# Projecting raw x in fp32 with centred weights in the first mixing stage of a hybrid layer

## The reference

```python
def _layernorm(x, axis=-1, eps=1e-05):
    m = jnp.mean(x, axis=axis, keepdims=True)
    v = jnp.var(x, axis=axis, keepdims=True)
    return (x - m) / jnp.sqrt(v + eps)

def _L0_attn_a_ref(x, W_q, W_k, W_v):
    Q = _l2norm(jnp.einsum('bnd,ed->bne', x, W_q))
    K = _l2norm(jnp.einsum('bnd,ed->bne', x, W_k))
    V = jnp.einsum('bnd,ed->bne', x, W_v)
    C = x.shape[1]
    global_feat = jnp.sum(K * V, axis=1, keepdims=True) / C
    return Q * global_feat

x = x + _L0_attn_a_ref(_layernorm(x, axis=-1), W_q, W_k, W_v)
x = x + _L0_ffn_ref(_layernorm(x, axis=-1), ...)
```

## Time and profile before

| what | us |
|---|---|
| median of 3 runs | 855.74 |
| lowest and highest run | 854.48, 856.68 |
| span of the profiled execution | 854.0 |
| TensorE busy (share) | 695.8 (81%) |
| VectorE busy | 576.9 (68%) |
| ScalarE busy | 515.5 (60%) |
| GpSimd busy | 480.7 (56%) |
| mean granted TensorE clock | 0.898 |

### The profile page before, as it was taken

One profiled execution on the slowest core, in us unless ns is written; L12 is line 12 of the kernel. 1 busy time (PEld: TensorE's weight loads), 2 busy tenths in 40 slices (PEclk: granted clock), 3 DMA queues, 4 the chain that ended last, 5 costly groups with the idle time before them and its releaser, 6 DMA issues.

```text
span 854.0 us, 22244 instructions
## 1 busy us (share of the span) xinstructions
PE 695.8 (81%) x7583; PEld 486.2 (57%) x7583; DVE 576.9 (68%) x1269; ACT 515.5 (60%) x1268; POOL 480.7 (56%) x501
## 2 busy tenths in 40 slices
PE   0663697898999957978898989988869798888888
PEld 0432686788888822333343434433238687877778
DVE  6699893766777376746986888975344256776646
ACT  3864874666666424746785878866453466766632
POOL 4995604677772478555177572166664336767640
PEclk9998599899999965887997999997568899999999
DMA  6222301232334142122122222121112212222217
GB/s 195 75 74 43 100 1 29 59 84 80 83 81 65 39 129 63 46 76 62 57 67 75 73 58 63 58 70 44 50 43 80 63 46 71 84 76 76 72 45 263
DMA packets 75810, 62.35 MB, mean 73 GB/s; under 512 B 11059, under 2 KB 68059, under 8 KB 75720
## 3 DMA queue, kind: packets, MB, share of 16 engines
q1 hardware_dynamic: 66632, 43.10, 17.6%
q0 software_dynamic: 9088, 17.98, 7.8%
HBM read 35.14 MB, written 26.68 MB: 72 GB/s over the span
## 4 chain that ended last, share of the span: by engine, by line
PE 52%; DVE 16%; ACT 10%; issue 8%; another core or an unknown queue 4%; DMA 3%; POOL 3%; SPq 1%; ACTq 0%; DVEq 0%; POOLq 0%
PE ps L995 25%; PE ps L1139 7%; PE ps L1382 7%; DVE mx L2431 5%; PE ps L1154 5%; ACT h L1591 3%; PE ps L1395 3%; DMA gy<-rows 2%; PE ps L1179 2%; POOL gy L840 2%; ACT xn L1504 1%; DVE xres L1903 1%; DVE stats L1813 1%; PE ps L1358 1%
## 5 line engine op out<-in xcount | busy, mean ns | idle before, releaser
L2431 DVE TENSOR_REDUCE mx<-ps 128x2 f32<-128x512 f32 x256 | 169.8, 684 | 62.5 <-PE ps L995 52.7
L1591 ACT ACTIVATE h<-ps,b1T 128x256 f32<-128x256 f32 x440 | 171.7, 478 | 59.3 <-PE ps L995 43.1
L1718 ACT ACTIVATE scratch<-ps 128x512 f32<-128x512 f32 x256 | 147.9, 599 | 71.4 <-PE ps L995 58.6
L995 PE MATMUL ps<-qkst 32*128 32x256 f16 x1024 | 112.6, 298 | 34.2 <-DVE mx L2431 23.6
L995 PE MATMUL ps<-xg,w1s 128*128 128x256 f16 x936 | 117.4, 276 | 23.4 <-issue 18.7
L799 POOL DMA_INDIRECT scratch<-rows,tok_i x78 | 90.3, 1157 | 70.6 <-DVE tok_i L2216 35.3
L942 POOL DMA_INDIRECT ytok<-yst,didx x78 | 92.1, 1181 | 58.1 <-DVE yst L2246 37.1
L1139 PE MATMUL ps<-w2s,hhi 128*128 x1248 | 118.6, 220 | 2.8 <-issue 1.7
L995 PEld LDWEIGHTS ps<-xg,w1s 128*128 x936 | 87.7, 99 | 38.3 <-issue 27.7
L1617 ACT ACTIVATE xg<-ps 128x512 f16<-128x512 f16 x78 | 46.5, 597 | 94.9 <-PE ps L1179 63.2
L2186 DVE SCALAR_TENSOR_TENSOR hlo<-h,hhi 128x1024 f16<-128x1024 f32 x78 | 95.6, 1225 | 2.7
(11 more groups left out here) (303 smaller groups left out, 1152.5 us busy)
## 6 DMA issues: line engine op xcount, KB each, us to landing
qkst<-qk SPq DMA_DIRECT2D x32, 256.0 KB
gy<-rows SPq DMA_DIRECT2D x39, 136.0 KB
ysorted<-yst SPq DMA_DIRECT2D x39, 128.0 KB
h<-in_L_ffn_ew SPq DMA_DIRECT2D x16, 256.0 KB, 3.1
qk<-hhi SPq DMA_DIRECT2D x32, 128.0 KB
xres<-in_L_attn_a_x SPq DMA_DIRECT2D x4, 512.0 KB, 6.1
rows<-hl SPq DMA_DIRECT2D x4, 512.0 KB, 3.1
qk<-hhi SPq DMA_DIRECT2D x32, 64.0 KB
```

What stands on the lines that cost most here:

```text
L995: return pe.matmul(o, a, b, start=start, stop=stop)
L1591: last = act.activation(h32[:, u % 2, f], HB[u % 2][:, f], ACT.Gelu_apprx_tanh, bias=b1T[:, ds(e * CH + c, 1)], scale=1.0 / PS)
L1718: act.activation(prb[:, (s // 4 * 4 + (s + 2) % 4) % 8, :], ps[:, s % 2, :], ACT.Exp, scale=HD ** -0.5 / (PS * PS))\
L2431: dve.tensor_reduce(mx[:, c, j:j + 2], ps[:, 2 + s % 2, :].rearrange("p (n k) -> p n k", n=2), AX_X, ALU.max).then_inc(Att.mx, 1)
```

## The change

The layer norm before mixing is linear but for the division by each token's deviation, so it is taken out of the projection. A weight's row minus its mean gives, on raw x, what the weight gives on x minus its mean: VectorE subtracts the means of the rows of W_q, W_k and W_v once (centre). TensorE turns raw x in fp32 (turn), ScalarE copies it out (copy_x), and project() is one fp32 matmul of 384 columns for each tile in place of three fp16 ones. The deviation cancels in q and k over their norms, but for the clamp, whose bound becomes a value for each token (least). For v it stays: 1/deviation (vscale) and 1/norm of k are multiplied (kscale), and that column, repeated 128 times, is the stationary operand of the mean's matmuls in place of ones, with 1/SEQ folded in. So k * v is a plain product of both tiles at once (products). norm(0) and its fp16 halves are gone.

Around it: the loops over batches are written out, pairs of batches share one root, clamp and inversion, and kv, qg and qvs have four buffers. W_q, W_k and W_v are loaded behind the first quarter of x. The other four weight matrices are turned at the end of mixing, and the low half of wbT is made by VectorE after routing; the bias halves and gate halves are made inside VectorE's mixing order. SyncE and GpSimd take the shared expert first, then experts 0 to 5; GpSimd then does the four additions to xres, and experts 6 and 7 after them. SyncE's bias stores stand between experts 5 and 6. The staging slots lie in vx in place of h32. TensorE's moe_blocks(0) waits for one expert's weights before the shared blocks and for all nine before the first routed block. The core of the diff, with eight columns of indentation cut:

```diff
-    for u in range(2):
-        expert(u, u, *two_of(u))
-    with sp.Fori(0, (E - 2) // 2) as i:
-        for u in range(2):
-            sp.wait_ge(ewt_used, 2 * i + u + 1)
-            expert(0, u, *two_of(2 * i + 2 + u))
+    expert(E, 0, sh_w1, sh_w2.rearrange("(c p) d -> p c d", p=P))
+    expert(0, 1, *two_of(0))
+    for e in range(1, E - 2):
+        sp.wait_ge(ewt_used, e)
+        expert(e, (e + 1) % 2, *two_of(e))
...
-    sp.wait_ge(ewt_used, E - 1)
-    expert(E, 0, sh_w1, sh_w2.rearrange("(c p) d -> p c d", p=P))
+    for e in range(E - 2, E):
+        sp.wait_ge(ewt_used, e)
+        expert(e, (e + 1) % 2, *two_of(e))
...
-    with pool.Fori(0, E // 2) as i:
-        for u in range(2):
-            split_expert(2 * i + u, u, 32 * (i + 1))
-    split_expert(E, 0, 32 * (E // 2 + 1))
+    split_expert(E, 0, 32, shared=True)
+    steps[0] += 3
+    with pool.Fori(0, E // 2 - 1) as i:
+        split_expert(2 * i, 1, 32 * (i + 1))
+        split_expert(2 * i + 1, 0, 32 * (i + 2))
+    for g in range(NG):
+        pool.wait_ge(Ln.hi, g + 1)
+        pool.tensor_tensor(group(xres, g), group(xres, g), group(xn, g), ALU.add).then_inc(Ln.added, 1)
+    split_expert(E - 2, 1, 32 * (E // 2))
+    split_expert(E - 1, 0, 32 * (E // 2 + 1))
+    steps[0] += 4 * E
+
+    pool.wait_ge(ewt_used, NE)
...
+        def turn(b):
+            if b % GB == 0:
+                pe.wait_ge(x_in[b // GB], 16)
+            if b >= 2:
+                pe.wait_ge(Ln.xT, b - 1)
             for c in range(CB):
+                last = pe.transpose(turned_x(b)[:, c * P:(c + 1) * P], xres[:, CB * b + c, :], ident32[:, :])
+            last.then_inc(Ln.turned, 1)
+
+        def mixing_weights():
+            pe.wait_ge(wa_made, 2)
+            for i in range(3):
+                last = pe.transpose(ps[:, 0, P * i:P * (i + 1)], wnat[:, i, :], ident32[:, :])
+            last.then_inc(wa_made, 1)
+
+        def other_weights():
+            pe.wait_ge(wnat_in, 5 * 16)
+            pe.wait_ge(Mix.kv, NBATCH - 1)
+            for i in range(4):
+                pe.transpose(WB[:, P * i:P * (i + 1)], wnat[:, 3 + i, :], ident32[:, :])
+            pe.transpose(B1, b1nat, ident32[0:NE * CH, 0:NE * CH]).then_inc(wT_turned, 1)
+
+        def project(b):
+            pe.wait_ge(Ln.xT, b + 1)
+            if b >= 2:
+                pe.wait_ge(Mix.kv, b - 1)
+            for c in range(CB):
+                last = mm(qkv_bank(b, c)[:, 0:3 * D], xT32[:, CB * b + c, :], wa32[:, :], True, True)
             last.then_inc(Mix.qkv, 1)
 
+        def mean(b):
             pe.wait_ge(Mix.kv, b + 1)
+            pe.wait_ge(Mix.inverse, 3 * (b // 2) + 3)
+            if b >= 2:
                 pe.wait_ge(Mix.qg, b - 1)
+            for c in range(CB):
+                at = CB * (b % 2) + c
+                last = mm(gate_bank(b), kscale[:, b // 2 % 2, at:at + 1].to_broadcast([P, P]),
+                          kv[:, b % 4, c, :], c == 0, c == CB - 1)
+            last.then_inc(Mix.mean, 1)
+
+        turn(0)
+        turn(1)
+        mixing_weights()
+        turn(2)
+        pe.wait_ge(wa_made, 4)
+        project(0)
+        turn(3)
+        project(1)
+        for p in range(NBATCH // 2):
+            for b in (2 * p, 2 * p + 1):
+                if b + 2 < NBATCH:
+                    project(b + 2)
+                if b + 4 < NBATCH:
+                    turn(b + 4)
+            if p == NBATCH // 2 - 1:
+                other_weights()
+            mean(2 * p)
+            mean(2 * p + 1)
...
+        def copy_x(b):
+            act.wait_ge(Ln.turned, b + 1)
+            act.activation(two(xT32, b), turned_x(b).rearrange("p (c n) -> p c n", c=CB), ACT.Copy)\
+                .then_inc(Ln.xT, 1)
+
+        def deviations():
+            act.wait_ge(Ln.var, 1)
+            act.activation(deviation[:, :], var[:, :], ACT.Sqrt, bias=epsq[:, 0:1], scale=SEQ * SEQ / D)\
+                .then_inc(Ln.by_act, 1)
+
+        def sums(b):
             act.wait_ge(Mix.qkv, b + 1)
+            if b >= 4:
+                act.wait_ge(Mix.qg, b - 3)
+            bank = qkv_banks(b)[:, :, 0:3 * D].rearrange("p c (j d) -> p c j d", d=D)
+            act.activation(qvs[:, b % 4, :, :, :], bank[:, :, 0:3:2, :], ACT.Copy)
             for c in range(CB):
                 for j in range(2):
+                    at = CB * (b % 2) + c
+                    last = act.activation(junk[:, 4 * (b % 2) + 2 * c + j, :], qkv_bank(b, c)[:, j * D:(j + 1) * D],
+                                          ACT.Square, accum_out=ssq[:, b // 2 % 2, at, j:j + 1])
             last.then_inc(Mix.ssq, 1)
+
+        def roots(p):
+            act.wait_ge(Mix.ssq, 2 * p + 2)
+            if p >= 2:
+                act.wait_ge(Mix.qg, 2 * p - 2)
+            act.activation(rnorm[:, p % 2, :, :], ssq[:, p % 2, :, :], ACT.Sqrt).then_inc(Mix.std, 1)
+
+        def other_weights():
+            act.wait_ge(wT_turned, 1)
+            act.activation(b1T[:, :], B1, ACT.Copy)
+            act.activation(wb32, WB, ACT.Copy, scale=WS)
+            act.activation(wbT[:, 0, :], WB, ACT.Copy, scale=WS).then_inc(wT_hi, 1)
+
+        copy_x(0)
+        copy_x(1)
+        act.wait_ge(wa_made, 3)
+        act.activation(wa32[:, :], ps[:, 0, 0:3 * D], ACT.Copy).then_inc(wa_made, 1)
+        copy_x(2)
+        for p in range(NBATCH // 2):
+            for b in (2 * p, 2 * p + 1):
+                sums(b)
+                if b == 0:
+                    copy_x(3)
+                    deviations()
+                if b % 2:
+                    roots(p)
+                if b + 4 < NBATCH:
+                    copy_x(b + 4)
+            if p == 1:
+                act.wait_ge(wnat_in, 5 * 16)
+                act.activation(gws[:, 0, :], gstage, ACT.Copy, scale=WS).then_inc(gate_split, 1)
+        other_weights()
...
+    def centre():
+        dve.wait_ge(wa_in, 3 * 16)
+        dve.tensor_reduce(wsum[:, :], wnat[:, 0:3, :], AX_X, ALU.add).then_inc(wa_made, 1)
+        dve.wait_ge(wa_made, 1)
+        dve.scalar_tensor_tensor(wnat[:, 0:3, :], over(wsum[:, :], 2, D), -1.0 / D, wnat[:, 0:3, :],
+                                 ALU.mult, ALU.add).then_inc(wa_made, 1)
...
+        def scales():
+            dve.wait_ge(Ln.by_act, 1)
+            dve.tensor_scalar(least[:, :], deviation[:, :], 1e-12 / SEQ, None, ALU.mult)
+            dve.reciprocal(vscale[:, :], deviation[:, :]).then_inc(Ln.rstd, 1)
+
+        def products(b):
+            dve.wait_ge(Mix.ssq, b + 1)
+            dve.tensor_tensor(kv[:, b % 4, :, :], qkv_banks(b)[:, :, D:2 * D], qvs[:, b % 4, :, 1, :], ALU.mult)\
+                .then_inc(Mix.kv, 1)
+
+        def invert(p):
+            ts = slice(2 * CB * p, 2 * CB * (p + 1))
+            n = rnorm[:, p % 2, :, :]
+            dve.wait_ge(Mix.std, p + 1)
+            if p == 0:
+                dve.wait_ge(Ln.rstd, 1)
+            dve.scalar_tensor_tensor(n, n, 1.0, over(least[:, ts], 2, 2), ALU.mult, ALU.max)\
+                .then_inc(Mix.inverse, 1)
+            dve.wait_ge(Mix.inverse, 3 * p + 1)
+            dve.reciprocal(n, n).then_inc(Mix.inverse, 1)
+            dve.wait_ge(Mix.inverse, 3 * p + 2)
+            dve.tensor_tensor(kscale[:, p % 2, :], n[:, :, 1], vscale[:, ts], ALU.mult).then_inc(Mix.inverse, 1)
+
+        def gated(b):
+            dve.wait_ge(Mix.mean, b + 1)
             for c in range(CB):
+                last = dve.scalar_tensor_tensor(qg[:, b % 4, c, :], qvs[:, b % 4, c, 0, :],
+                                                rnorm[:, b // 2 % 2, CB * (b % 2) + c, 0:1],
+                                                gate_bank(b), ALU.mult, ALU.mult)
+            last.then_inc(Mix.qg, 1)
+
...
+        for g in range(NG):
+            dve.wait_ge(x_in[g], 16)
+            for b in range(GB * g, GB * (g + 1)):
+                tile_stats(b)
+            if g == 0:
+                centre()
+        dve.wait_ge(Ln.stats, NBATCH)
+        merge_moments(0)
+        products(0)
+        scales()
+        products(1)
+        invert(0)
+        for p in range(NBATCH // 2):
+            b = 2 * p
+            ahead = p + 1 < NBATCH // 2
             if ahead:
+                products(b + 2)
+            gated(b)
+            if p > 0:
+                moments(b - 1)
+            add(b)
             if ahead:
+                products(b + 3)
+            gated(b + 1)
+            moments(b)
+            add(b + 1)
+            if p == 0:
+                split_biases()
+            if p == 3:
+                gate_lo()
             if ahead:
+                invert(p + 1)
         moments(LAST)
...
-        pe.wait_ge(ewt_used, NE)
+        pe.wait_ge(ewt_used, 1)
...
         turn(1, 1, 0)
+        pe.wait_ge(ewt_used, NE)
         es = list(experts(0, 4))
...
             invert()
             weigh_all()
+            dve.wait_ge(wT_hi, 1)
+            dve.tensor_tensor(wbT[:, 1, :], wb32, wbT[:, 0, :], ALU.subtract).then_inc(wT_lo, 1)
             gathered()
```

(65 more changed lines are left out.)

213 lines of the change are left out of this document (74 added, 139 removed).

## The result

| | before | after |
|---|---|---|
| median of 4 runs, us | 856.21 | 867.36 |
| lowest and highest | 854.48, 857.19 | 864.33, 871.39 |
| span of the profiled execution | 854.0 | 865.7 |
| TensorE busy in it | 695.8 | 708.6 |
| VectorE busy | 576.9 | 559.6 |

After over before is 1.0122 (95% interval 1.0091 to 1.0152): 1.2% slower, 867.4 us where 843.0 was forecast and 851 was the end of the range. Every ratio here is of fast runs alone, and on the chip of e1 to e4 the kernel before takes 772.7 us in the median of its nine fast runs, 776.0 in that of all nineteen.

What follows compares the result with a forecast made beforehand. VectorE, held in step by GpSimd's instructions, was taken as the bound in mixing. 17.4 us gained there less 4.5 lost later gave 12.9 net: 855.7 - 12.9 = 842.8, given as 843, range 835 to 851.

Steps and rivals of the forecast that it cites:

- What bounds the kernel before: Mixing: VectorE is the bound, its instructions with two SBUF operands waiting for GpSimd's; 5.93 us per pair of batches.
- my doubt: Routing: perhaps only scalar_tensor_tensor is held by GpSimd's reads, three of seven instructions; return some 1.5 us, not 4.3.
- The start: Before mixing: the first layer norm's work goes, and the first gated() comes at 18.7 us, 2 us either side.
- The pace of a pair: Mixing: VectorE 4.4, TensorE 4.5, ScalarE 3.7 us of work, but GpSimd's boundaries keep a pair at 5.94 us.
- GpSimd's stretch: Weight splits beside mixing: from 17.75 us, shared expert and experts 0 to 5, to 57.3; bias stores cost nothing.
- The end of mixing: Second norm's merge at 64.4 us against 81.81, a gain of 17.4 us.
- Routing: Splits of experts 6 and 7 beside routing hold VectorE's two-operand instructions: 4.3 us lost, ends 0 and 11.
- (4): Mixing: TensorE's fp32 work at its lower clock becomes the bound, pair 9.0 us, 7.4 slower, 863; chance 0.08.
- (3): Mixing: VectorE isn't held in step, pairs take 4.4 us, gain 27.5, total 832.7; chance 0.07.
- (1): Routing: no collision with GpSimd, so the 4.3 us stay, total 838.5; chance 0.14.
- (2): Start of mixing: weights' path delays the first product, or pairs need a seventh GpSimd boundary; 5 us lost, 848; chance 0.15.
- The net of the forecast: Whole kernel: 17.4 us gained to the end of mixing, less 4.5, gives 12.9 us.

Runs made afterwards that it cites:

- e1: Changed kernel with TensorE turning x of batch b + 4 before projecting batch b + 2, not after; 0.9974 of the kernel before.
- e4: Changed kernel with filler matmuls of zeros on TensorE before every projection from batch 3 on; 1.0164 of the kernel before.
- e8: e5 with GpSimd waiting for the end of mixing before it splits any expert; mixing ends at 51.4 us, one run.
- e9: e6 with expert 6 split before the additions to xres and expert 7 after them; 840.14 us, 0.9812 of the kernel before.
- e2: Changed kernel with GpSimd splitting experts 6 and 7 before the four additions to xres; 1.0108 of the kernel before.
- e6: e5 with e2's order and the bias stores spread two by two behind the loads of experts 2 to 7; 843.10 us, 0.9815 of before.
- e7: Changed kernel with filler matmuls of zeros on TensorE before the odd batches' projections alone; 860.38 us, 1.004 of the kernel before.
- e5: e1 with ScalarE copying x of batch b + 3, not b + 4, behind the sums of batch b; 843.93 us, 0.9846 of before.
- e3: Changed kernel with both edits, e1's turn first and e2's splits first; 0.9926 of the kernel before.

## Why the prediction was wrong

**What bounds the kernel before** was read rightly as far as it went: e8 and e9 show that GpSimd's reads hold VectorE's instructions with two SBUF operands, and for the changed kernel what they cost. In routing the rule of the Trainium skill that the prediction weighed (SBUF — State Buffer, Who interferes with whom) holds against my doubt: tensor_tensor is held too (0.81 in after, 0.43 in e2). That the closing memset would hold nobody came true for instructions with two SBUF inputs (e9), not for all: in after a tensor_scalar begun at 117.36 beside the memset took 1.00 us, where the next one took 0.23. It was off the path.

**The start** failed twice by the same circle. ScalarE was to go from the deviations straight to sums(1), at 14.3. But copy_x(4) stands between them, and its turn(4) stands behind project(2), which waits for products(0). From the chain of after:

```profile
15.38 0.23 PE ps L1064 x2
...
15.63 0.38 ACT xn L1577
16.02 0.49 ACT gy L1590
```

So products(1) came at 17.57 in place of 15.8, and the two means at 19.72 in place of 18.0. Then gated(0) stands behind products(2) in VectorE's order, and that is a turn of the circle later: 22.20. I had followed the queues of this part and left out copy_x(4), and I stopped one instruction of VectorE too early. e1 gives 18.28.

**The pace of a pair** is the step that made the forecast wrong. "VectorE 4.4, TensorE 4.5, ScalarE 3.7 us" were sums of each engine's work, and the pace was taken as the largest, or GpSimd's. They were near (a free pair takes 4.2 in e8), but a largest sum is a lower bound. No term followed one batch through all four queues, though the diff has what is needed: two sets of PSUM banks, turn(b + 4) behind project(b + 2), copy_x(b + 4) ahead of the next sums(). It could have been costed blind from the prediction's own figures: products 0.35, project 1.35, turn 0.45, copy 0.27 and sums 1.5 come to 3.9 a batch, 7.8 a pair, well over 5.94. In the forecast's own sum, 18.7 + 7 x 7.8 + 3.0, mixing would have ended at 76.3 and the program taken about 855 us: no gain, though not yet the loss that was measured.

**GpSimd's stretch** ended at 58.97, forecast 57.3. It began 1.5 us earlier (16.22) and lost 4.41 waiting for expert 5's weights. I had costed the bias stores at nothing since they precede expert 6's load alone. But they also follow expert 5's load in the same queue: issued by 43.8, it let GpSimd go at 53.1, where such loads take 3.1 in the median; in the second profile GpSimd waited 1.78. In e6 and e9, with the stores spread, that wait is gone. Pairs are as long beside it as without it in after, so it cost nothing there.

**The end of mixing**, 64.4, came out as 84.7. From 84.7 to 81.2 is the clock, as far as e7 gives it back (4.9 us by the second profile); from 81.2 to e5's 63.3, 17.9 us, is the order of calls at a clock near full. Together that is 21.4, 1.1 more than the 20.3 that were missed, since e5 ends 1.1 ahead of the forecast.

**Routing** was right in kind, and its size came out near partly by luck: rank 3.6 us later after routing's start, forecast "4 us later". The two held instructions that the forecast had behind rank weren't held (0.59 us at 121.68: the splits had ended). What was missed is 1.5 us in the rank matmuls themselves, 3.23 against 1.74: the granted clock is 0.50 between 116.0 and 119.3, where it was 1.00 before. TensorE was busy for 6.67 of the 6.72 us ahead of rank before, and for 6.48 of 10.31 in after. 5.2 us in all up to the gather, forecast 4.3, and 0.2 behind it, as forecast for wbT.

**The rivals.** (4) said slower, by TensorE at its lower clock, pair 9.0 and mixing end 84.7, the measured value to the digit. It is not confirmed by that. It wanted a busy TensorE at the lower level all through; the clock was 0.78, TensorE was idle for a third of the time, and at a clock of 0.94 (e7) only 3.5 us come back. The low clock was a result of the waits. Its argument against itself, that TensorE would be busier than before, was the same mistake: a circle leaves it idle. (3), no lock, falls with e5 and e8; its 832.7 also kept a routing loss that without a lock would not be there. (1) falls with e2. (2) had the start 5 us late by way of the weights' loads; it was 3.5 late by the circle.

The net of the forecast, 12.9 us, is near what e5 measures (857.92 - 843.93 = 14.0): the terms were sound for a program in the right order, and wrong for this one. That e5 comes within 1 us of the 843.0 is partly luck, for it has the clock's 1.5 us in routing, which the forecast left out, and a shorter mixing by the late weights; in e6 and e9, where GpSimd never waits for them, mixing ends at 64.6 and 64.5.

## What to carry to other kernels

Sums of work per engine bound a pipelined loop from below; before they are taken as the pace, follow one item through every queue, writing down for each instruction what stands ahead of it in its engine's order as well as what it waits for, and price each closed circle. Where a profile shows a stretch with no engine full, read the chain of waits over one period: the engine and line that come back are the circle, and an instruction in it that isn't wanted yet (here a turn and a copy for three batches later) is the one to move. Splitting work that reads SBUF on GpSimd belongs beside stretches where VectorE isn't the bound: it cost 11.9 us in mixing (e8), 5.2 in routing with the clock's part (e2) and 2 to 3 in the norm (e3, e6).

## What the runs showed of the hardware

- TensorE's clock fell to its lower level (0.50, 1.2 GHz) behind pauses of 2.5 us, again and again, in a stage where it was busy for 19.5 of 31 us: project() 1.53 and 2.9 us by turns. The Trainium skill (TensorE: Matmul & The Clock Gate, A second HAM failure mode: psum-queue depth-cycling) tells of a kernel whose small pauses while PSUM banks come free let the clock swing between its two levels; the trace agrees, with longer pauses, and filling them with matmuls of zeros (e7) held it at 0.94.
- Loads of 256 KB take 3.1 us in the median. Two of them, issued at 42.99 and 43.36 with twelve small stores behind them in their queue, let GpSimd go only at 53.13, though the 173 GB/s between 43 and 46 amount to their 512 KB, and from 46 on 3 GB/s moved. In the second profile of the same kernel it was 50.49. That the stores were the reason rests on e6 and e9 alone, where they were spread and the wait was gone; how they held it is open.
- Two fp32 matmuls of 384 columns take 1.53 us, 0.77 each, where 0.67 was worked out from the 0.22 of a 128-column one.
- The stationary operand that is one column repeated costs no more than a full matrix: two means take 1.06 us, where one with the matrix of ones took 0.71.
- The kernel before took 763.4 to 782.0 us on one chip and 853.7 to 861.3 on another. TensorE is idle for 5.5 to 5.7 us ahead of the first routed block in the profiles of before, after, e5 to e9, 146.09 to 151.73 in the kernel before, with no releaser in the profile, and not in those of e1 to e4, which come from the first chip. What the difference between the chips is stays open.
- A tensor_scalar of 8 columns took 1.00 us beside a memset by GpSimd, 0.17 to 0.23 otherwise, while instructions with two SBUF inputs kept their 0.42 beside one. Why the one was held and not the others isn't shown.
